# Four-layer transformer: the first work of the last two attentions placed inside the two-expert layer's last group, and the convolution matrices' transfers placed in mid-attention

## The reference, cut to what matters

```python
x = x + tanh(g_xattn[0]) * L0_xattn(layernorm(x), ctx)     # 16 heads
x = x + tanh(g_ffn[0])   * L0_ffn(layernorm(x))            # one of 8 experts for each token
x = x + tanh(g_xattn[1]) * L1_xattn(layernorm(x), ctx)     # top 32 of 64 scores, then a convolution over 64 tokens
x = x + tanh(g_ffn[1])   * L1_ffn(layernorm(x))            # 8 experts, 7 of them equal: two are computed
x = x + tanh(g_xattn[2]) * L2_xattn(layernorm(x), ctx)     # 8 heads of 64
x = x + tanh(g_ffn[2])   * L2_ffn(layernorm(x))            # ternary weights
x = x + tanh(g_xattn[3]) * L3_xattn(layernorm(x), ctx)     # 8 heads of 64
x = x + tanh(g_ffn[3])   * L3_ffn(layernorm(x))
```

## Time and profile before

| | |
|---|---|
| median of 3 runs | 1495.56 us (1492.52 to 1497.89) |
| the profiled execution's own time | 1483.07 us |
| its span | 1481.3 us |
| mean granted TensorE clock | 0.954 |
| busy share PE, PEld, DVE, ACT, POOL | 89%, 68%, 74%, 61%, 48% |
| first attention, to 380 us | PE busy 358.05 of 380 |
| routed experts alone, 380 to 463 | PE 55.53, DVE 24.60 of 83 |
| second attention and convolution, 463 to 760 | DVE 269.43, PE 225.11 of 297 |
| its feed-forward part, 760 to 838 | DVE 68.53, PE 63.98 of 78 |
| two-expert layer, 838 to 977 | PE 137.07 of 139, DVE 55.75 |
| decoder, from 977 | PE 477.00, DVE 374.83 of 504 |

### The profile page before, as it was taken

How to read it: one execution, slowest core, us unless ns; L and a number is a source line. 1 busy time by engine, 2 the same in 40 slices (tenths; PEclk the granted TensorE clock), 3 DMA queues, 4 the chain that set the end, 5 groups by cost and what they waited for, 6 DMA issues and landing times.

```text
span 1481.3 us, 49260 instructions
## 1 busy us (share of the span) xinstructions
PE 1316.7 (89%) x17517; PEld 1010.4 (68%) x17517; DVE 1091.5 (74%) x4511; ACT 907.4 (61%) x1996; POOL 706.6 (48%) x1359
## 2 busy tenths in 40 slices
PE   6999999999857687887877899989999999999997
PEld 5888888888644344444545667657777777788885
DVE  5878878887424699999989733437888998866664
ACT  5666666666535577787323444545788888855553
POOL 3655555577464688766456411123433433343330
PEclk9999999999878799899989899979999999999999
DMA  8050000000455401000030100000000000000000
GB/s 191 3 128 0 0 0 2 3 28 15 143 172 147 96 19 29 1 0 1 2 68 1 37 1 0 0 1 2 3 2 0 0 3 3 2 10 7 7 15 23
DMA packets 67152, 43.15 MB, mean 29 GB/s; under 512 B 24746, under 2 KB 63492, under 8 KB 66884
## 3 DMA queue, kind: packets, MB, share of 16 engines
q1 hardware_dynamic: 58628, 33.97, 9.3%
q0 software_dynamic: 2048, 4.20, 1.0%
q10 hardware_dynamic: 6336, 3.15, 0.7%
HBM read 28.71 MB, written 12.58 MB: 28 GB/s over the span
## 4 chain that ended last, share of the span: by engine, by line
PE 34%; DVE 17%; issue 8%; ACT 6%; POOL 5%; DMA 2%; SPq 1%; DVEq 0%; ACTq 0%; POOLq 0%
PE ps L2349 4%; PE ps L2340 4%; PE ps L2679 4%; DVE arena L1710 4%; PE ps L2686 3%; DVE arena L1704 3%; PE ps L2760 3%; PE ps L2673 2%; PE ps L2740 2%; PE ps L2748 2%; PE ps L2729 2%; PE ps L2832 2%; DMA arena<-f_outs,arena 1%; DVE xn L678 1%; PE ps L2801 1%
## 5 line engine op out<-in xcount | busy, mean ns | idle before, releaser
L3192 POOL TENSOR_TENSOR arena<-arena 128x512 f32<-128x512 f32 x64 | 67.8, 1059 | 111.2 <-DVE arena L3116 111.2
L1710 DVE MATCH_REPLACE8 arena<-arena 128x64 f32<-128x64 f32 x512 | 101.6, 207 | 0.5 <-issue 0.2
L2202 DVE TENSOR_SCALAR_CACHE_REDUCE thr_hits<-thr_abs,thr_candidate 128x512 bf16<-128x512 f32 (+1 forms) x248 | 101.7, 475 | 0.0
L2679 PE MATMUL ps<-arena,toeplitz 96*128 96x128 f32 x512 | 71.9, 284 | 9.9 <-ACT arena L2911 5.2
L1704 DVE MAX8 arena<-arena 128x8 f32<-128x64 f32 x512 | 75.7, 209 | 2.9 <-issue 2.0
L2349 PEld LDWEIGHTS ps<-arena,toeplitz 128*128 128x128 f32 x512 | 63.4, 192 | 21.0 <-issue 12.8
L2414 ACT ACTIVATE toeplitz<-ps,arena 128x512 f32<-128x512 f32 x64 | 42.1, 684 | 57.9 <-PE ps L2340 57.8
L616 POOL TENSOR_TENSOR arena<-arena 128x1024 f32<-128x1024 f32 x32 | 61.4, 1918 | 32.3 <-DVE arena L557 31.1
L538 DVE TENSOR_REDUCE arena<-ps 128x16 f32<-128x1024 f32 x32 | 39.1, 1222 | 49.5 <-PE ps L357 49.4
L2679 PEld LDWEIGHTS ps<-arena,toeplitz 96*128 96x128 f32 x512 | 63.5, 195 | 15.6 <-issue 9.5
L386 PEld LDWEIGHTS ps<-arena 128*64 128x64 f32 x1024 | 60.3, 139 | 19.2 <-issue 11.0
(11 more groups left out here) (471 smaller groups left out, 4197.9 us busy)
## 6 DMA issues: line engine op xcount, KB each, us to landing
toeplitz<-ssm_toeplitz_scratch SPq DMA_DIRECT2D x2, 2048.0 KB, 18.2
arena<-L_ffn_packed SPq DMA_DIRECT2D x24, 128.5 KB, 3.2
toeplitz<-L_ffn_packed SPq DMA_DIRECT2D x24, 128.5 KB, 2.2
f_rows<-arena SPq DMA_DIRECT2D x2, 1536.0 KB, 9.5
f_outs<-arena ACTq DMA_DIRECT2D x12, 256.0 KB, 2.8
ssm_toeplitz_scratch<-ssm_padded_kernel SPq DMA_DIRECT2D x1, 2048.0 KB, 12.6
out<-x_res SPq DMA_DIRECT2D x8, 256.0 KB, 2.3
arena<-ctx SPq DMA_DIRECT2D x2, 768.0 KB, 6.1
```

The source lines that it names most:

```text
L1710: ins = V.match_replace(W2[:, s, h, :], m8[:, r, h, :], src[:, s, h, :], TAKEN)
L2202: ins = V.tensor_scalar(self.hits[:, j, at:at + n], self.abs[:, at:at + n], self.cand[:, c:c + 1].bitcast(F32), 0.0, ALU.is_ge, ALU.add, a ...
L2679: last = T_.matmul(ps[:, 0, c * P:(c + 1) * P], weights[phase].k[0:DC, c * P:(c + 1) * P], cg[0:DC, s, :], start=True, stop=True)
L3192: G_.tensor_tensor(probs, probs, rc[:, s, :].unsqueeze(2).to_broadcast([P, heads, CTX]), ALU.mult).then_inc(s_prob.sem, 1)
```

## The change

It has two parts that have nothing to do with each other.

**Transfers.** `sp_matrices` waits for one semaphore more, `rows_taken`, which is `route.x_done` at its end: all 32 gathered tiles have been added.

**The seam between the two-expert layer and the decoder.** The decoder's prologues are cut out and handed to `ffn1` as `k.dec_first`, which runs them in group 7 only (`else` of `if more`). DVE and POOL do both first norms there, after DVE's router weights and a wait for group 0. PE transposes tile 0 behind `hidden(7)`, into bank 6 in place of bank 1, does the first keys between `outputs(6)` and `outputs(7)`, and the first queries behind `outputs(7)`. ACT scales the four gated weights one by one behind the GELUs of units 0 to 3, and behind the last GELU copies transpose and keys, runs one small exponential on a scratch column (`table_preload`), and copies the queries. The waits for `before` stay ahead of each engine's first step.

```diff
--- before.py
+++ after.py
@@ -1390,6 +1390,7 @@
     def sp_matrices(self, e):
         e.wait_ge(self.summed.sem, 3)
         e.wait_ge(self.toep_free.sem, self.toep_free.end)
+        e.wait_ge(self.rows_taken.sem, self.rows_taken.end)
 
         windows = self.padded[:, self.L - 1:2 * self.L - 1]
         windows = bass.AP(windows.tensor, windows.offset, [windows.ap[0], [-1, SEQ], [1, SEQ]])
@@ -2377,8 +2378,12 @@
             hidden(e, g, 1)
             for u in range(2, U):
                 hidden(e, g, u)
-                if u == U - 1 and more:
-                    turn_x(e, g + 1)
+                if u == U - 1:
+                    if more:
+                        turn_x(e, g + 1)
+                    else:
+                        e.wait_ge(l_read.sem, l_read.end)
+                        k.dec_first["pe_turn"](e)
                 if u == 5:
                     turn_weights(e, g)
                 outputs(e, g, u - 2)
@@ -2387,7 +2392,11 @@
             outputs(e, g, U - 2)
             if more:
                 logits(e, g + 1)
+            else:
+                k.dec_first["pe_keys"](e)
             outputs(e, g, U - 1)
+            if not more:
+                k.dec_first["pe_queries"](e)
 
         pipelined_groups(e, body)
 
@@ -2412,8 +2421,12 @@
                 x, c = divmod(u, C)
                 e.wait_ge(h_full.sem, h_full.at(U * g + u + 1))
                 nc.scalar.activation(hT[:, u % 3, :], ps[:, u % 3, :], ACT.Gelu_apprx_tanh, bias=b1[:, x, c:c + 1]).then_inc(h_laid.sem, 1)
+                if not more and u < 4:
+                    k.dec_first["act_gate"][u](e)
             if more:
                 copy_x(e, g + 1)
+            else:
+                k.dec_first["act"](e)
 
         pipelined_groups(e, body)
 
@@ -2482,6 +2495,9 @@
             if more:
                 ln.dve_aggregate(e, g + 1, True)
                 ln.dve_apply(e, g + 1, g + 1)
+            else:
+                e.wait_ge(x_done.sem, x_done.at(1))
+                k.dec_first["dve"](e)
             for x in range(E):
                 add_expert(g, x)
             e.wait_ge(b_full.sem, b_full.at(g + 1))
@@ -2512,6 +2528,9 @@
             if more:
                 ln.pool_rstd(e, g + 1)
                 rstd_router(e, g + 1)
+            else:
+                e.wait_ge(before.sem, before.end)
+                k.dec_first["pool"](e)
 
         pipelined_groups(e, body)
 
@@ -2663,9 +2682,9 @@
         e.wait_ge(out_done.sem, out_done.at(16 * GROUPS))
 
 
-    def turn_xn(e, t, s):
+    def turn_xn(e, t, s, bank=1):
         e.wait_ge(xn_done.sem, xn_done.at(t + 1))
-        T_.transpose(ps[:, 1, 256:256 + P], xn[:, s, :], k.ident[:]).then_inc(xt_full.sem, 1)
+        T_.transpose(ps[:, bank, 256:256 + P], xn[:, s, :], k.ident[:]).then_inc(xt_full.sem, 1)
 
     def queries(e, t, s, phase):
         e.wait_ge(xt_laid.sem, xt_laid.at(t + 1))
@@ -2839,15 +2858,12 @@
             e.wait_ge(w.loaded.sem, w.loaded.at(w.count))
             e.wait_ge(w_gated.sem, w_gated.at(4))
         e.wait_ge(before.sem, before.end)
-        keys(e, 0, 0, 0)
-        turn_xn(e, 0, 0)
-        queries(e, 0, 0, 0)
         steps(e, lambda t, r, b: pe_step(e, t, r, b))
 
 
-    def copy_xn(e, t, s):
+    def copy_xn(e, t, s, bank=1):
         e.wait_ge(xt_full.sem, xt_full.at(t + 1))
-        S.copy(xnT[:, s * P:(s + 1) * P], ps[:, 1, 256:256 + P]).then_inc(xt_laid.sem, 1)
+        S.copy(xnT[:, s * P:(s + 1) * P], ps[:, bank, 256:256 + P]).then_inc(xt_laid.sem, 1)
 
     def copy_queries(e, t):
         e.wait_ge(q_full.sem, q_full.at(t + 1))
@@ -2865,12 +2881,17 @@
         e.wait_ge(v_full.sem, v_full.at(t + 1))
         S.copy(VH[:, s, :, :, :].rearrange("p b c d -> p (b c d)"), ps[:, 5, :]).then_inc(v_laid.sem, 1)
 
-    def gate_weights(e):
-        for i, w in enumerate(weights):
-            g = GATES[i]
-            e.wait_ge(w.loaded.sem, w.loaded.at(w.count))
-            S.activation(w.o, w.o, ACT.Copy, scale=k.gates[:, g:g + 1]).then_inc(w_gated.sem, 1)
-            S.activation(w.bo, w.bo, ACT.Copy, scale=k.gates[:, g:g + 1]).then_inc(w_gated.sem, 1)
+    def gate_weights(e, i):
+        w, g = weights[i // 2], GATES[i // 2]
+        e.wait_ge(w.loaded.sem, w.loaded.at(w.count))
+        part = (w.o, w.bo)[i % 2]
+        S.activation(part, part, ACT.Copy, scale=k.gates[:, g:g + 1]).then_inc(w_gated.sem, 1)
+
+    def act_first(e):
+        copy_xn(e, 0, 0, 6)
+        copy_keys(e, 0)
+        S.activation(k.preload[:], k.half[:, 0:1], ACT.Exp)
+        copy_queries(e, 0)
 
     def act_weights(e, r):
         if r == 4:
@@ -2937,11 +2958,7 @@
         S.activation(r3[:, (r - F3) % 2, :], ps[:, hbank(r), :], ACT.Relu).then_inc(r3_done.sem, 1)
 
     def act(e):
-        gate_weights(e)
         e.wait_ge(before.sem, before.end)
-        copy_keys(e, 0)
-        copy_xn(e, 0, 0)
-        copy_queries(e, 0)
         steps(e, lambda t, r, b: act_step(e, t, r, b))
 
 
@@ -3146,14 +3163,16 @@
         e.wait_ge(r3_done.sem, r3_done.at(t - F3 + 1))
         V.tensor_tensor(hT3[:, slot, :], ps[:, hbank(r), :], r3[:, slot, :], ALU.mult).then_inc(h3_laid.sem, 1)
 
-    def dve(e):
-        e.wait_ge(before.sem, before.end)
+    def dve_first(e):
         for t in range(2):
             norm_stats(t, t)
         for t in range(2):
             norm_aggregate(e, t, t)
         for t in range(2):
             norm_apply(e, t, t)
+
+    def dve(e):
+        e.wait_ge(before.sem, before.end)
         steps(e, lambda t, r, b: dve_step(e, t, r, b))
 
 
@@ -3191,14 +3210,22 @@
             probs = PR[:, s, :, :, :].rearrange("p c m j -> p (c m) j")
             G_.tensor_tensor(probs, probs, rc[:, s, :].unsqueeze(2).to_broadcast([P, heads, CTX]), ALU.mult).then_inc(s_prob.sem, 1)
 
-    def pool(e):
-        e.wait_ge(before.sem, before.end)
+    def pool_first(e):
         for t in range(2):
             ctx_copy(e, t, t)
         for t in range(2):
             norm_rstd(e, t, t)
+
+    def pool(e):
+        e.wait_ge(before.sem, before.end)
         steps(e, lambda t, r, b: pool_step(e, t, r, b))
 
+    def pe_first_keys(e):
+        e.wait_ge(weights[0].loaded.sem, weights[0].loaded.at(weights[0].count))
+        keys(e, 0, 0, 0)
+
+    k.dec_first = dict(pe_turn=lambda e: turn_xn(e, 0, 0, 6), pe_keys=pe_first_keys, pe_queries=lambda e: queries(e, 0, 0, 0),
+                       act_gate=[lambda e, i=i: gate_weights(e, i) for i in range(4)], act=act_first, dve=dve_first, pool=pool_first)
     return dict(sp=sp, pe=pe, act=act, dve=dve, pool=pool), dict(sp=sp_store)
 
 
@@ -3212,7 +3239,7 @@
         loaded = k.x_ready
         route = RoutedExperts(k, io)
         route.loaded = loaded
-        k.ssm.toep_free = route.o_full
+        k.ssm.toep_free, k.ssm.rows_taken = route.o_full, route.x_done
         new()
         weights0 = dict(q="L0_xattn_Wq", k="L0_xattn_Wk", v="L0_xattn_Wv", o="L0_xattn_Wo", bo="L0_xattn_bo")
         attn0, sp_keys, sp_values = attention_heads(k, io, weights0, 0, k.thresholds, k.ssm, late, route)
```

## The result

The changed kernel takes 1474.64 us in the median of 4 runs (1473.63 to 1481.86), the kernel before 1495.67 us in 4 runs beside them; the ratio is 0.9874 with a 95% interval of 0.9842 to 0.9906. The medians differ by 21.0 us, and the ratio makes 18.8 us of 1495.67. Predicted were 19.0 us and 1476.6, with a range of 1472.0 to 1485.5.

A forecast was written before the change was run, and what follows sets the result against it. It took DVE's 11.29 us wait for a gather beside the matrix loads and the chained waits at the seam as the limits. 11.0 + 3.4 + 4.6 = 19.0 us off the 1495.56 median gave 1476.6, range 1472 to 1485.5.

The forecast's parts named there:

- The sum: Whole kernel: 11.0 us from the matrices, 3.4 and 4.6 from the seam, together 19.0 us faster.
- The matrices: Second attention: DVE's 11.29 us wait for a gather beside the two matrix loads goes, gaining 11.0 us.
- The change doesn't do what it says: Rival, second attention: the gather was late for its own cause, leaving 8.0 us alone, 1487.6; 4%.
- What it costs later: Delayed matrices before the convolution: ready at about 613.6, 103 us of cover, so costing nothing.
- The matrices hit something else: Rival: moved transfers delay an instruction fetch at the DVE and POOL loop, giving 1490.2 or 1481.1; 10%.
- slower: Rival, same loop entry: three instruction packets each late by up to 13.6 us; two full ones give 1503.8; 3%.
- The seam, group 7: Two-expert layer's group 7: moved work delays the last sum by 1.3 for gate scalings, 0.95 keys, 0.1 transpose.
- The seam gives nothing: Rival, group 7: gate scalings delay PE at each first unit, added 2.35 grow to 8, leaving 1484.6; 8%.
- From the last sum to the first maximum: Seam into decoder: scores start at once, maximum 0.9 us behind the last sum, arriving 3.4 us earlier.
- The two first steps: Decoder steps 0 and 1: preloaded table and held clock cut 18.43 us to 13.84, gaining 4.6.
- that case: Rival, decoder steps 0 or 1: the clock falls again, those steps gain only 1.6 us, total 1479.6; 27%.
- The cause given for the fall: Seam: TensorE's fall to 1.2 GHz followed idle 976 to 980; PE without a gap removes its cause.

The follow-up runs named there:

- e2: Kernel after without the added `rows_taken` wait, so the seam alone; 1486.06 us, ratio 0.9967.
- e8: Kernel before with six products that nobody reads in TensorE's idle time at the seam, nothing moved; 1479.42 us, ratio 0.999.
- e9: Kernel after without the added `rows_taken` wait, the seam alone run again in the third batch; 1472.59 us, ratio 0.9926.
- e10: Kernel after without the added wait, plus twelve unread products in PE's gaps of decoder steps 0 and 1; 1474.17 us, ratio 0.9938.
- e4: Kernel before with only the two matrix loads waiting for `rows_taken`, the store left where it was; 1483.79 us, ratio 0.994.
- e5: Kernel before with each matrix load cut into eight pieces of 16 channels, at the old time; 1472.55 us, ratio 0.9952.
- e7: Kernel after with the four gate scalings behind the GELUs of units 3 to 6 instead of 0 to 3; 1461.23 us, ratio 0.9869.
- e6: Kernel after without the small exponential, so the table load stands ahead of the decoder's first exponential; 1471.62 us, ratio 0.9943.
- e12: Kernel after, unedited, run a third time in the third batch; 1465.09 us, ratio 0.9868.
- e3: Kernel after, unedited, run again in the first batch; 1474.49 us, ratio 0.9885.

## Why the prediction was right

**The sum.** Predicted 19.0 us; measured 18.8 by the ratio (21.0 by the medians), 17.2 and 19.6 in the other two batches (0.9885 of 1492.51, 0.9868 of 1482.27). The parts alone gave 9.0 for the matrices and 4.9 and 11.0 for the seam (0.9967 of 1492.51, 0.9926 of 1482.27); with the mean of these two, 17.0 together, which the intervals don't tell from 19. The time itself, 1476.6 predicted and 1474.64 measured, hangs on carrying the gain over to the median.

**The matrices, 11.0 us predicted.** A without the wait, in five traces (before, e2, e8, e9, e10), is 262.0 to 266.3, mean 264.1; with it, in eight, 252.2 to 256.7, mean 254.1. So 10.0 us. All waits of DVE for gathered rows together tell the same: 13.4 to 14.3 us without the added wait, 3.8 to 4.3 with it, 9.7 less in the mean. The prediction took the one long wait away and left the others as they were; they grew from 2.7 us to 3.8, which is about the 1 us that it had too much. The cause was the two loads, as the prediction read from landings and queue; e4 shows it. Its "took turns" fits e5, where smaller pieces took most of the wait away. That it is one single wait holds for three traces (11.3, 11.2 and 11.0 us); in e8 and e10 it is two, 7.6 and 2.9 us, and 7.0 and 3.2 us, ahead of two pairs beside the same loads. *The change doesn't do what it says* (4%) is refuted.

**What it costs later, nothing predicted.** The wait ended at 590.25, the slower load landed after 23.2 us as before, at 625.4: 102 us ahead of the convolution, 103 predicted. DVE was busy 34.55 of 36 us beside the loads, three instruction packets among them, and no gather kept it waiting over 0.6 us. *The matrices hit something else* (10%) and *slower* (3%) did not come. What the prediction did not see is SP's issue of the small loads, 15.69 us behind the large ones; nobody waits for it.

**The seam, group 7.** The last sum moved from 15.66 to 17.72 us behind group 6's, so 2.06; predicted 2.35 = 1.3 + 0.95 + 0.1. e7 splits it: 1.05 for the gate scalings (1.3 predicted), 1.01 for keys and transpose (1.05 predicted). *The seam gives nothing* (8%) is refuted.

**From the last sum to the first maximum.** 0.9 predicted, 1.18 measured: the scores start 0.42 us behind the end of the sum, not at once. By the code PE waits for that sum's semaphore ahead of them; the trace puts the wait down to ACT's copy, which ended 0.24 us earlier, at 979.43. The two small errors cancel by luck: the maximum gained 3.46 us, 3.4 predicted.

**The two first steps.** This term was mis-sized. Predicted 13.84 us from the 6.92 of the twelve later steps; with the clock held they take 11.85, since steps 0 and 1 lack work that later ones have (from the third to the fourth maximum it is 6.25 us already; in the kernel before it was 1008.42 - 1002.16 = 6.26, so the row that shows the mean of 6.92 to be too long for the first steps was there to read). So 6.6 us in place of 4.6 where the clock holds. Where it falls, C is 16.64 and the gain 1.8, near the 1.6 that the prediction gave for that case. Chance 27% given, two of eight seen, or two of six without the fillings: too few to test it.

**The cause given for the fall** was only half right: "the clock's fall that followed the idle 976 to 980 has lost its cause". e8 filled the idle time and the clock fell later, in step 0; e6 has the seam as the change leaves it, but the table load in step 0, and fell too. The change removed two gaps, the seam's and the table load's, and neither alone kept the clock up in the one profile of each. The preload was worth 1.4 us directly and 4.3 through the clock in e6. With the gaps that remain (1.49 us ahead of the scores, 1.17 in step 0) the clock fell in e2 and e12 and held in after, e3, e7 and e9.

With six of eight held, A, B and C give 10.0 + 3.5 + (0.75 x 6.6 + 0.25 x 1.8 = 5.4) = 18.9 us. That this meets the 19.0 is luck in part: the matrices were set 1.0 us too high and the first steps 0.8 too low.

**The profile's own 9.2 us.** The prediction carried the gain over from a profile that lay 12.5 us below its median and said that no row explained it. The traces after show where such a distance can lie: the start of the second attention varies from 463.4 to 477.2. That it lay there in the runs of the median is not shown, since they have no trace.

**Open.** How much of e5's gain is the size of the packets. What decides in a given execution whether the clock falls in step 0; why SP's issue among the routed experts takes 9 us in some executions and 2 in others; whether filling the gaps keeps the clock up.

## What to carry to other kernels

A large transfer that nobody needs soon belongs behind the small ones that an engine is waiting for, and where it can't be moved, smaller pieces get most of it back (here eight times as many packets: a wait of 3.7 us in place of 11.3, and 7.1 us of gain against 9.0). At a seam between two parts count the clock as well as the waits: the load of a table was 1.3 us by its row, and the two steps were 5.7 us longer with it, with what the clock did behind it. And cut two traces at common places before comparing them, since stretches that the change never touches moved by up to 14 us here.
